# A two-convolution block and a spline on one core: x added by DMA in the spline stage, six result buffers, Horner form, no loops

## The reference

```
w = sign(w)                                  # both 3x3 weights
h = relu(batchnorm(conv3x3(x, w1)))
y = batchnorm(conv3x3(h, w2))                # statistics over images and pixels
z = relu(y + x)
u = (clip(a*z + b, -1.5, 1.5) + 1) * 15.5    # place on the knots of a spline
out = id_gain*z + sum_r mix[c,r]*spline_r(u) + bias
```

## Time and profile before

| what | value |
|---|---|
| median of 3 runs | 1256.31 us (1255.05 to 1257.22) |
| profiled execution | 1254.66 us, of it the span 1252.8 us |
| VectorE (DVE) busy | 1062.8 us, 85% |
| TensorE (PE) busy | 1058.6 us, 85% |
| ScalarE (ACT) busy | 868.8 us, 69% |
| GpSimd (POOL) busy | 113.4 us, 9% |
| first convolution, second, spline | up to about 214, 424 and 1253 us of the span |

### The profile page before, as it was taken

The page is one execution under the profiler, slowest core; times in us unless marked ns, Lnnn a source line. Parts: engine busy times, 40 slices in busy tenths (PEclk is TensorE's granted clock), DMA queues, the critical chain, the costliest instruction groups (busy, mean ns, idle before and its releaser), DMA issues. The chain is left out here.

```text
span 1252.8 us, 51454 instructions
## 1 busy us (share of the span) xinstructions
PE 1058.6 (85%) x23562; PEld 710.2 (57%) x23562; DVE 1062.8 (85%) x951; ACT 868.8 (69%) x424; POOL 113.4 (9%) x189
## 2 busy tenths in 40 slices
PE   6999996999999368887888788878887888788876
PEld 4688885788888234554545455444544545455444
DVE  5765656766666689999999999999999999999987
ACT  4454544777787267688868877887788778877881
POOL 6000000282000000000000000000000000000000
PEclk9999998999999778998989889898998989889898
DMA  7666766576777386677767766777677667776552
GB/s 227 259 257 256 276 255 225 217 277 252 271 264 300 136 235 181 183 216 194 185 189 213 196 181 193 208 192 184 189 214 192 184 197 206 194 182 197 157 114 78
DMA packets 58215, 260.85 MB, mean 208 GB/s; under 512 B 16336, under 2 KB 16336, under 8 KB 50000
## 3 DMA queue, kind: packets, MB, share of 16 engines
q1 hardware_dynamic: 52528, 230.88, 56.3%
q0 software_dynamic: 4608, 25.69, 11.0%
q10 hardware_dynamic: 928, 1.90, 0.6%
HBM read 104.29 MB, written 77.07 MB: 145 GB/s over the span
## 5 line engine op out<-in xcount | busy, mean ns | idle before, releaser
L1181 PE MATMUL tab<-edge_mask,diag 128*32 128x392 bf16 x10240 | 501.8, 358 | 132.6 <-DVE poly L1090 130.8
L1181 PEld LDWEIGHTS tab<-edge_mask,diag 128*32 128x32 f16 x10240 | 281.7, 104 | 339.0 <-DVE poly L1090 143.4
L982 ACT ACTIVATE edge_mask<-cell,thr 128x6272 bf16<-128x6272 bf16 x62 | 338.5, 5508 | 0.0
L711 PE MATMUL acc<-split,w 64*64 64x392 f16 x4608 | 195.9, 329 | 12.0 <-DVE w L463 10.8
L711 PE MATMUL acc<-band_split,w 64*64 64x392 f16 x4608 | 197.9, 330 | 9.4 <-ACT band_split L368 7.2
L410 ACT ACTIVATE yout<-acc 128x1568 f32<-128x1568 f32 x64 | 94.2, 1473 | 160.6 <-PE acc L711 139.4
L1181 PE MATMUL tab<-middle_mask,diag 128*32 128x392 bf16 x4096 | 183.4, 332 | 25.0 <-DVE middle_mask L1052 25.0
L711 PEld LDWEIGHTS acc<-band_split,w 64*64 64x64 f16 x4608 | 164.1, 107 | 42.9 <-issue 14.1
L711 PEld LDWEIGHTS acc<-split,w 64*64 64x64 f16 x4608 | 155.3, 107 | 51.9 <-issue 12.6
L520 DVE BATCH_NORM_STATS2 stats<-yout 128x392 f32 (+1 forms) x240 | 118.0, 555 | 60.2 <-ACT yout L410 59.4
L930 ACT ACTIVATE zbuf<-lin,cst 128x1568 f32<-128x1568 f32 x32 | 54.3, 1697 | 163.8 <-DVE lin L1016 157.9
(11 more groups left out here) (126 smaller groups left out, 816.9 us busy)
## 6 DMA issues: line engine op xcount, KB each, us to landing
y_scratch<-yout SPq DMA_DIRECT2D x32, 1568.0 KB, 6.2
cell<-cell SPq DMA_DIRECT2D x496, 98.0 KB, 3.3
xin<-y_scratch SPq DMA_DIRECT2D x16, 1568.0 KB, 9.0
zbuf<-y_scratch SPq DMA_DIRECT2D x32, 784.0 KB, 5.9
lin<-in_x SPq DMA_DIRECT2D x32, 784.0 KB, 6.1
lin<-far POOLq DMA_DIRECT2D x32, 784.0 KB, 8.8
out<-lin SPq DMA_DIRECT2D x31, 784.0 KB, 4.1
xin<-in_x SPq DMA_DIRECT2D x15, 1568.0 KB, 9.3
```

Of the source, the lines that this page charges most:

```text
L711: mm = pe.matmul(acc[h * C:(h + 1) * C, 2 * k + r, 0:TILE], weights[part][own, tap * C:(tap + 1) * C], image[own, first:first + ROWS, dx:d ...
L982: act.activation(mask_of(b, q)[:, :, :], cell4[b % 2][:, :, :], ACT.Sign, bias=thr[:, q:q + 1]).then_inc(sign_mask_ready, 1)
L1181: mm = pe.matmul(tab[(b + t) % 2][j * GROUP:(j + 1) * GROUP, sub, 0:SUB], keep["diag"][part][:, j % 2, t, q, :], mask_of(b, q)[:, j, sub * ...
```

## The change

- `total` stays on VectorE for the first four chunks only. For these SP loads y and x ahead, in the last pair of the second convolution.
- From chunk 4 on, SP loads y into lin (four chunks ahead), ScalarE's new `scale` multiplies it in place, and GpSimd's new `add_x` adds x from DRAM with an accumulating DMA. `position` waits for that DMA.
- lin has six buffers. SP's order is load, spread, store. Its last wait for the stores moves from the end of `convolutions` into `spline`, behind the copies of the first two chunks.
- `distance_square`, `near_part`, `slope` and `add_slope` go. The polynomial is in Horner form: square table added, times d, linear table added, times d.
- `finish` of c-1 stands behind `near_cube` and `linear`. On ScalarE `distance` stands between the two edge masks.
- The second chunk's copies are all issued by SP, where ScalarE issued half.
- The loops are written out. An early activation on ScalarE is `Sqrt` where it was `Identity`.

```diff
-BUFS = 4
+LIN = 6
+AHEAD = 4
...
                 if n == 2 * half_rounds - 1:
-                    sp.wait_ge(stored[0], 16 * (half_rounds + 1))
-                    for half in range(2):
...
+                    for c in range(AHEAD):
+                        px = slice(c % 2 * CHUNK, (c % 2 + 1) * CHUNK)
+                        sp.wait_ge(stored[c // 2], 16 * (half_rounds + 1))
+                        y_to, x_to = keep["opening"](c)
+                        sp.dma_start(y_to[:, :], y2[c // 2][:, px]).then_inc(keep["y_loaded"][c], 16)
+                        sp.dma_start(x_to[:, :], x[c // 2][:, px]).then_inc(keep["x_loaded"][c], 16)
...
-            for b in range(2):
-                sp.wait_ge(stored[b], 32 * half_rounds)
...
-            act.activation(tmp[:, 5:6], row_scale[:, 0:1], ACT.Identity)
+            act.activation(tmp[:, 5:6], row_scale[:, 0:1], ACT.Sqrt)
...
+            def load(c):
+                if c < LIN:
+                    sp.wait_ge(sum_ready, AHEAD)
+                wait_past(sp, stored[c % LIN], 16 * (c // LIN))
+                sp.dma_start(lin_of(c)[:, :], image_half(y2, c)).then_inc(y_loaded[c % LIN], 16)
...
+            spread(0)
+            spread(1)
+            for b in range(2):
+                sp.wait_ge(keep["y_stored"][b], 16 * PAIRS)
+            for c in range(CHUNKS):
+                if c + 4 < CHUNKS:
+                    load(c + 4)
+                if c + 2 < CHUNKS:
+                    spread(c + 2)
+                if c > 0:
+                    store(c - 1)
...
+            def add_x(c):
+                pool.wait_ge(scaled, c - AHEAD + 1)
+                pool.dma_start(lin_of(c)[:, :], image_half(x, c), accum_op=ALU.add).then_inc(x_added, 16)
...
             for c in range(CHUNKS):
+                if AHEAD <= c + 3 < CHUNKS:
+                    add_x(c + 3)
                 add_far(c)
...
+            def scale(c):
+                act.wait_ge(y_loaded[c % LIN], 16 * (c // LIN + 1))
+                act.activation(lin_of(c)[:, :], lin_of(c)[:, :], ACT.Identity, scale=cc(BN2_S)).then_inc(scaled, 1)
+            def position(c):
+                if c < AHEAD:
+                    act.wait_ge(sum_ready, c + 1)
+                else:
+                    act.wait_ge(x_added, 16 * (c - AHEAD + 1))
+                if c >= 2:
+                    act.wait_ge(offset_ready, c - 1)
+                    act.wait_ge(cell_ready, c - 1)
...
+            for c in range(CHUNKS):
+                far_distance(c)
+                if c + 2 < CHUNKS:
+                    position(c + 2)
+                if AHEAD <= c + 3 < CHUNKS:
+                    scale(c + 3)
+                far_square(c)
+                if c + 2 < CHUNKS:
+                    cells(c + 2)
+                if c + 1 < CHUNKS:
+                    edge(c + 1, EDGE_QUADS[0])
+                    distance(c + 1)
+                    edge(c + 1, EDGE_QUADS[1])
...
+            def times_offset(c, t, done):
+                dve.wait_ge(table_used, used(c, t))
+                dve.scalar_tensor_tensor(out=poly[c % 2][:, :], in0=offset[c % 2][:, :], scalar=1 / POINT,
+                                         in1=poly[c % 2][:, :], op0=ALU.mult, op1=ALU.mult).then_inc(done, 1)
...
+            for c in range(2):
+                fixed(c)
+                offsets(c)
+                linear(c)
+                total(c + 2)
             first_masks()
+            for c in range(CHUNKS):
+                if c > 0:
+                    add_table(c - 1, T_VAL, slope_ready, c)
+                if c + 2 < CHUNKS:
+                    fixed(c + 2)
+                near_cube(c)
+                if c + 2 < CHUNKS:
+                    linear(c + 2)
+                if c > 0:
+                    finish(c - 1)
+                far_cube(c)
+                far_part(c)
+                if c + 1 < CHUNKS:
+                    for q in MIDDLE_QUADS:
+                        middle(c + 1, q)
+                add_table(c, T_SQ, table_used, used(c, T_NEAR))
+                times_offset(c, T_SQ, near_ready)
+                add_table(c, T_LIN, near_ready, c + 1)
+                times_offset(c, T_LIN, slope_ready)
+                if c + 2 < CHUNKS:
+                    offsets(c + 2)
```

More of the change, by code:

```diff
@@ L824, in quarters, with summed @@
             return t[:, :].rearrange("p (q x) -> p q x", q=4)
[L826 to L844, removed]
+        def summed(c, t):
+            return tab[(c + t) % 2][:, :, 0:SUB]
@@ L857, in _, with used, image_half, lin_of @@
+        def used(c, t):
+            return TABLES * c + t + 1
+        def image_half(t, c):
+            return t[c // 2][:, (c % 2) * CHUNK:(c % 2 + 1) * CHUNK]
+        def lin_of(c):
+            return lin[c % LIN]
         @block.sync
         def _(sp):
[L859 to L871, removed]
@@ L887, in store @@
[L887 to L903, removed]
@@ L1070, in far_cube, with base, near_cube @@
-            def far_cube(i, b):
-                c = BUFS * i + b
+            def base(c, t):
+                return (keep["plain"] if c == 0 else first)[:, t:t + 1]
+            def near_cube(c):
+                dve.wait_ge(far_ready, c + 1)
+                dve.wait_ge(table_ready, used(c, T_NEAR))
+                dve.scalar_tensor_tensor(out=quarters(poly[c % 2]), in0=summed(c, T_NEAR), scalar=base(c, T_NEAR),
+                                         in1=quarters(poly[c % 2]), op0=ALU.add, op1=ALU.mult).then_inc(table_used, 1)
@@ L1134, in closing_quarters @@
                                              op1=ALU.add).then_inc(table_used, 1)
-                    dve.wait_ge(table_used, used(last, b, T_VAL) + sub)
-                    dve.scalar_tensor_tensor(out=lin[b][:, own], in0=poly[b % 2][:, own], scalar=cc(AMP),
-                                             in1=lin[b][:, own], op0=ALU.mult, op1=ALU.add).then_inc(whole, 1)
-            total(0, 0)
-            total(0, 1)
-            fixed(0, 0)
-            offsets(0, 0)
-            linear(0, 0)
@@ L1144, in _ @@
-            fixed(0, 1)
-            offsets(0, 1)
-            linear(0, 1)
-            first_masks()
-            def body(i, b, n):
-                previous, following, after = exists(n, b - 1), exists(n, b + 1), exists(n, b + 2)
-                if previous:
-                    add_table(i, b - 1, T_VAL, slope_ready, 2 * (BUFS * i + b - 1) + 2)
-                    finish(i, b - 1)
-                if after:
-                    total(i, b + 2)
-                near_cube(i, b)
-                if after:
-                    fixed(i, b + 2)
-                    linear(i, b + 2)
-                far_cube(i, b)
-                far_part(i, b)
-                if following:
-                    for q in MIDDLE_QUADS:
-                        middle(i, b + 1, q)
-                add_table(i, b, T_SQ, table_used, used(i, b, T_NEAR))
-                near_part(i, b)
-                slope(i, b)
-                add_slope(i, b)
-                if after:
-                    offsets(i, b + 2)
@@ L1172, in _ @@
-            rounds(dve, body)
+                    dve.wait_ge(table_used, used(c, T_VAL) + sub)
+                    dve.scalar_tensor_tensor(out=lin_of(c)[:, own], in0=poly[c % 2][:, own], scalar=cc(AMP),
+                                             in1=lin_of(c)[:, own], op0=ALU.mult, op1=ALU.add).then_inc(whole, 1)
+            total(0)
+            total(1)
+            for c in range(2):
+                fixed(c)
+                offsets(c)
+                linear(c)
+                total(c + 2)
```

264 lines of the change are left out of this document (100 added, 164 removed).

## The result

The changed kernel takes 1235.38 us in the median (1234.23 to 1236.81, 4 runs), the kernel before 1256.37. The ratio is 0.9834, 95% interval 0.9817 to 0.9851: 21 us less, where 27 were forecast.

The account below looks back on a forecast made before the run. VectorE bounds narrowly, then a TensorE-VectorE ring of 24.15 us a chunk: -25.8 us over 31 periods, opening -0.3, square root -0.7, closing +0.2, together -26.6 from 1254.66, with 1.65 run offset said as 1229; range 1215 to 1246.

Parts of the forecast that it names:

- VectorE's busy share: Spline stage, VectorE busy 731 of 750 us; the rival reading keeps VectorE the bound: period 23.2, some 1200 us, chance 0.04.
- the ring: Per chunk: TensorE's value, near, far tables, then VectorE's `far_cube`, `far_part`, two masks, square addition; 24.4 us, forecast 24.15.
- rival (B): Value table on TensorE keeps its 5.4 us cases: mean 4.74, ring 24.62, about 1244 us; chance 0.17.
- VectorE's sum: VectorE's own work per chunk: 24.92 us before, 23.2 after `total` leaves and the order changes.
- `near_cube` by 828.7 and the linear table "ahead of 823.12": Trace times in one chunk: `near_cube` waits until about 828.7; linear table used at 822.56, before the near table's 823.12 start.
- x by DMA at 0: GpSimd's accumulating DMA of x: +1.9 us of DMA time a chunk, no engine waiting for it, 0 us in time.
- Rival (C): DMA ring through the landing of `far`, ScalarE and VectorE: 21.8 us; delayed, period 26.1, about 1290 us; chance 0.05.
- 5 us from deciding: Distance claimed for the `far` DMA ring if the skill's 3.8 us estimate for 0.80 MB held; measured 8.8 contradicts it.
- Opening and closing: Spline's start: shorter store wait against two more `total`s, -0.3 us, bounds -3.1 and +1.8; its end: one more dependency, +0.2.
- the root: First square root on ScalarE: its table load goes, shortening VectorE's 0.98 us wait; -0.7 us.
- Horner form, order of `finish`, six buffers, no loops: Horner and `offsets` dependencies +0.19 and +0.06, `finish` -0.20 us a chunk on VectorE; six buffers suffice; no loops 0.

Follow-up runs that it names:

- experiment 1: The kernel before with only `total` removed from the third chunk on (y is loaded but not added): 1233.9 us, ratio 0.982.
- experiment 2: The changed kernel with one more VectorE instruction a chunk, directly before `far_cube`: 1234.74 us, ratio 0.9837.
- experiment 3: The changed kernel with one more VectorE instruction a chunk, behind `far_part`: 1258.49 us, ratio 1.0022 to the kernel before.
- experiment 4: The changed kernel with the two middle masks behind the linear table's addition and the edge masks first in near and far tables: 1219.88 us, ratio 0.9717.
- experiment 6: The changed kernel with the linear table computed twice on TensorE, 64 matmuls more a chunk: 1217.96 us, ratio 0.9712.
- experiment 9: Experiment 5 with two buffers for `far` used in turn: 1182.51 us, ratio 0.9417.
- experiment 7: The changed kernel without GpSimd's accumulating DMA of x from the fifth chunk on (x not added): 1234.79 us, ratio 0.9836.
- experiment 11: The changed kernel with two buffers for `far` and nothing else: 1237.44 us, ratio 0.9862.
- experiment 5: Experiment 4 with `offsets` behind the value table's addition instead of ahead of it: 1203.24 us, ratio 0.9585.
- experiment 10: The kernel before, `total` still on VectorE, with the mask order of experiment 4: 1259.31 us, ratio 1.0031.

## Why the prediction was right, and where it was off

- *The bound.* That VectorE's busy share misleads and the ring takes over at 24.4 us was right: 24.31 measured, waits for TensorE in every chunk, and experiments 1 to 4 and 6 give it from several sides. The two closing chunks of the kernel before had told it: with no `total` in them they already ran at 24.4.
- *The term that was mis-sized is the ring's.* I took 24.15, between 23.98 and 24.4, on the ground that 5.4 us for the value table stands only behind an idle of 4.39. In the changed kernel the idle is at most 3.90 and 5.42 occurs 4 times in 31, so the idle time does not decide that; without these the mean of 4.45 would be 4.30. The 31 periods brought -20.8 instead of -25.8 us, 5.0 of the 6.4 us between 1229 and 1235.4 (in the range). The 5.4 us were also the sign named for rival (B). With a mean of 4.74 and 1244 it lay on the other side, so the truth is a mixture of the two.
- *VectorE's sum.* 23.2 summed, at most 23.0 measured. It didn't count here, but it made the expectation of experiment 9 too small.
- *`near_cube` by 828.7 and the linear table "ahead of 823.12"*: right at 4.1 us and more for the value table. Experiment 6 shows that this second way round takes over at 23.7, which the prediction didn't carry further.
- *x by DMA at 0.* Right, by experiment 7. The estimate for its load was right too: 1.9 us a chunk, 0.08 of the DMA engines' time; their share in the stage rose from 0.72 to 0.82 (for the same stretch as the earlier trace rows). That `far` might land later did not happen: 8.3 us against 8.8.
- *Rival (C)* did not decide here (experiment 11), and does at 22.65 us (experiments 5 and 9). Its 21.8 us, with the 9.8 of experiment 5 for the landing, are 22.8. The "5 us from deciding", said of a landing of 3.8 us, is a slip: against the 11.1 us from which (C) decides it is 7.3, and 5 us is the distance from the 8.8 of the rows. The Trainium skill ("SBUF — State Buffer", the trap that VectorE blocks DMA) has GpSimd kept from writing descriptors while VectorE is in a fast mode. The trace agrees by the issue of `far`: 1.59 us in the changed kernel, where the middle masks run beside it, and 0.86 in experiment 4, where they don't. The rows agree closer than in the sign: in the changed kernel the issue ends 0.12 us behind the end of the first of the two masks in all 31 chunks, and again in experiment 3, where the masks begin 0.5 us later and the issue takes 2.07. It did not reach the time.
- *Opening and closing.* -0.3 was forecast for the opening and -0.1 came (-2.1 at the stage's end, +1.9 to the masks, +0.1 behind them); the root gave its 0.7. The 1.4 us lost in the second convolution are within what executions differ by.
- *Horner form, order of `finish`, six buffers, no loops*: nothing by themselves, as forecast; shown only together, by experiment 1.

## What to carry to other kernels

Before taking work from an engine, add up every ring of waits that passes through it and other engines: the gain ends where the next ring begins, and a chunk at the edge of the loop that already lacks the work may show its length. Then take work out of the ring rather than off the engine: moving the two masks and `offsets` and doubling one buffer brought 53 us more (1182.5 us), where removing an instruction had brought 21. An order that is worth nothing in one state of the kernel can be worth much after the next change, so it should be tried again.

## What was not expected of the hardware

What TensorE's clock adds to a ring does not follow from the idle time alone. In the changed kernel the same 64 matmuls, behind the same idle of 3.90 us, took 4.09 to 5.42 us in a recurring sequence, 4.45 on average at a period of 24.31 us. In experiment 3, at 25.05 us and an idle of 4.38, it was another sequence with 4.71 on average. Behind 2.5 us of idle (experiment 4) and behind 3.76 (experiment 10) the clock had fallen in some chunks and not in others. What sets the sequence stays open, since period and idle changed together. Redundant matmuls in the idle time kept it at 2.4 GHz and made the kernel 17 us faster. Taking 0.8 MB a chunk of accumulating DMA off GpSimd's queue left the landing of its other transfer unchanged (8.4 against 8.3 us).
